# Narrow attention: one bank for the last four heads' queries and keys, and one maximum over the rows of two heads

## The reference

```
q = (x @ wq).reshape(b, n, heads, 16)    # heads = 20
k = (ctx @ wk).reshape(b, j, heads, 16)
v = (ctx @ wv).reshape(b, j, heads, 16)
a = softmax(q k^T * 16 ** -0.5)          # 512 x 512 per head
out = (a v) @ wo + bo
```

## Time and profile before

| | |
|---|---|
| median of 3 runs | 3327.07 us (3326.29 to 3332.21) |
| the profiled execution | 3336.34 us, its span 3334.6 us |
| PE busy | 3214.7 us, 96% of the span |
| DVE / ACT / POOL busy | 1737.4 / 1476.5 / 805.1 us |
| run r3, first column product at | 1817.8 us |
| run r7, first column product at | 2982.4 us |
| a self round (round 1), 1904.2 to 1994.7 | 90.5 us |
| a cross round (round 5), 2260.2 to 2347.3 | 87.1 us |

### The profile page before, as it was taken

How to read it: one execution, slowest core, us unless ns; L and a number is a source line. 1 busy time by engine, 2 the same in 40 slices (tenths; PEclk the granted TensorE clock), 3 DMA queues, 4 the chain that set the end, 5 groups by cost and what they waited for, 6 DMA issues and landing times.

```text
span 3334.6 us, 39289 instructions
## 1 busy us (share of the span) xinstructions
PE 3214.7 (96%) x15478; PEld 1462.8 (44%) x15478; DVE 1737.4 (52%) x2568; ACT 1476.5 (44%) x1983; POOL 805.1 (24%) x620
## 2 busy tenths in 40 slices
PE   7999999999999999999999999999999999989997
PEld 3344344443434343435444344444434545643443
DVE  2645455454555555552234677777762222656664
ACT  3544444445454545441112656666652112326664
POOL 2544444454554554550000000000000000000000
PEclk9999999999999999999999999999999999989999
DMA  3000000000100000000000000000002000000000
GB/s 110 24 16 20 16 17 20 23 19 20 58 18 18 17 23 13 16 24 20 0 5 26 1 1 1 30 11 6 1 23 65 1 0 33 1 5 6 14 9 17
DMA packets 37284, 62.32 MB, mean 19 GB/s; under 512 B 7024, under 2 KB 24944, under 8 KB 36208
## 3 DMA queue, kind: packets, MB, share of 16 engines
q1 hardware_dynamic: 37104, 59.82, 5.9%
HBM read 57.19 MB, written 2.62 MB: 18 GB/s over the span
## 4 chain that ended last, share of the span: by engine, by line
PE 89%; DVE 5%; ACT 4%; issue 1%; POOL 0%; DMA 0%; ACTq 0%; DVEq 0%; POOLq 0%
PE bank L1589 9%; PE bank L510 9%; PE bank L595 9%; PE bank L1126 7%; PE bank L737 5%; PE bank L351 5%; PE bank L673 5%; PE bank L1059 4%; PE bank L1251 3%; PE bank L676 3%; PE bank L709 3%; PE bank L1276 3%; PE bank L1179 2%; PE bank L533 2%; DVE heads L1084 2%; PE bank L1594 2%
## 5 line engine op out<-in xcount | busy, mean ns | idle before, releaser
L1084 DVE TENSOR_REDUCE heads<-bank 128x1 f32<-128x512 f32 x960 | 598.3, 683 | 237.2 <-PE bank L1072 236.4
L544 DVE TENSOR_REDUCE heads<-bank 128x2 f32<-128x1024 f32 x320 | 392.4, 1226 | 594.7 <-PE bank L533 594.7
L581 POOL TENSOR_TENSOR heads<-heads,probs 128x1024 f32<-128x1024 f32 x160 | 389.5, 2434 | 12.5
L567 ACT ACTIVATE probs<-bank 128x1024 f32<-128x1024 f32 x320 | 328.0, 1025 | 130.3 <-PE bank L519 130.0
L577 POOL TENSOR_TENSOR heads<-probs 128x1024 f32<-128x1024 f32 x80 | 190.7, 2384 | 712.8 <-ACT probs L567 712.8
L510 PE MATMUL bank<-heads 64*128 64x512 f32 x1280 | 335.7, 602 | 0.1
L1059 PE MATMUL bank<-heads 32*128 32x512 f32 x1920 | 296.8, 628 | 25.8 <-ACT weights L1097 10.9
L595 PE MATMUL bank<-probs,values 128*64 128x512 f32 x1280 | 294.0, 601 | 1.4 <-ACT nmT L558 1.0
L1589 PE MATMUL bank<-hT,weights 128*128 128x512 f32 x640 | 291.8, 606 | 1.5 <-issue 1.5
L1097 ACT ACTIVATE weights<-bank 128x1024 f32<-128x1024 f32 x236 | 228.8, 1022 | 96.0 <-PE bank L1059 93.9
L1652 ACT ACTIVATE ctx_in<-bank,b_col 128x512 f32<-128x512 f32 x80 | 55.1, 688 | 419.4 <-PE bank L1594 323.8
(11 more groups left out here) (205 smaller groups left out, 4868.9 us busy)
## 6 DMA issues: line engine op xcount, KB each, us to landing
heads<-in_wqk SPq DMA_DIRECT2D x40, 320.0 KB, 2.8
heads<-in_wqk SPq DMA_DIRECT2D x40, 256.0 KB, 2.6
weights<-in_L_xattn_w_ff SPq DMA_DIRECT2D x3, 1600.0 KB, 7.2
weights<-in_L_xattn_ff_w SPq DMA_DIRECT2D x3, 1600.0 KB, 7.1
ctx_in<-in_ctx SPq DMA_DIRECT2D x12, 384.0 KB, 3.7
weights<-in_L_xattn_qkv_q SPq DMA_DIRECT2D x2, 1632.0 KB, 7.4
weights<-in_L_xattn_wo SPq DMA_DIRECT2D x2, 1600.0 KB, 12.2
x_res<-in_x SPq DMA_DIRECT2D x4, 640.0 KB, 13.3
```

Of the source, the lines that this page charges most:

```text
L544: nc.vector.tensor_reduce(v["negm"][:, U % 2, qb, :].rearrange("p (g k) -> p g k", g=2)[:, :, 0], M.ROWS[:, :, :], AX.X, ALU.max, negate=T ...
L567: nc.scalar.activation(v["probs"][:, kb, :, :], M.COLS[kb % 2][:, :, :], ACT.Exp, scale=float(r.work[n][0].prm["dh"]) ** -0.5).then_inc(r. ...
L581: nc.gpsimd.tensor_tensor(ps, ps, pr[:, k, :, :], ALU.add).then_inc(r.sem("part"), 1)
L1084: nc.vector.tensor_reduce(v["negm"][:, tile, qb, 32 * h + at:32 * h + at + 1], r.bank_of(item, m)[:, :], AX.X, ALU.max, negate=True).then_ ...
```

## The change

Two things change, and with them the way banks are dealt out.

**Queries and keys of the last unit together.** Q2 and K2 become one item QK2 at step 0. Its products take 64 columns of wq into partitions 0 to 63 and 64 columns of wk into partitions 64 to 127 of the same bank, in turn (`QK_pe4`). ScalarE makes both tiles by four instructions on 64 partitions, and only the last of them releases the bank (`QK_act4`). V3 moves from step 0 to step 2, and what waited for K2 now waits for V3.

**Rows of two heads together.** A row item is now a pair of heads: two products into the two banks of a pair, one release to VectorE behind the second, and one maximum over 128 x 1024 that writes two values and releases both banks.

**Banks.** Banks 4 and 5 are pair 0, banks 6 and 7 pair 1. At step i the first row pair goes to pair i % 2, the second to the other, and the extra items alternate between the two single banks of pair i % 2. Counters: free0 to free3 for single banks, free4 and free5 for the pairs. A single item waits for its bank's counter and the pair's; a pair waits for its own and both single ones.

```
-    return [(f"row{i // 4}_{i % 4}_{h}", n) for h in range(4)] if 0 <= n < r.N else []
+    return [(f"row{i // 4}_{i % 4}_{p}", n) for p in range(2)] if 0 <= n < r.N else []
...
+        def choose(self, name, i):
+            if name[0:3] == "row":
+                self.large = 0
+                return 4 + (i + int(name[7])) % 2
+            self.large = 1 - self.large
+            return 2 * (i % 2) + 1 - self.large
+
+        def shares(self, bank):
+            return ((4,), (4,), (5,), (5,), (0, 1), (2, 3))[bank]
...
             self.wait(pe, f"free{bank}", k)
+            for other, count in self.beside[item, n]:
+                self.wait(pe, f"free{other}", count)
...
             if i == 0 and now:
-                items += [("Q2", n), ("V3", n)]
+                items += [("QK2", n)]
...
             if i == 2 and now:
-                items += [("K2", n)]
+                items += [("V3", n)]
...
+                r.wait_free(pe, item, m)
+                for g in range(2):
+                    strip = slice(64 * p + 32 * g, 64 * p + 32 * g + 32)
+                    last = nc.tensor.matmul(r.bank_of(item, m)[:, g, :], v["QB"][strip, u, qb * P:qb * P + P], v["KB"][strip, u, :], start=True, stop=True)
+                last.then_inc(r.full(item, m), 1)
...
-                nc.vector.tensor_reduce(v["negm"][:, tile, qb, 32 * h + at:32 * h + at + 1], r.bank_of(item, m)[:, :], AX.X, ALU.max,
-                                        negate=True).then_inc(r.free(item, m), 1)
+                out = v["negm"][:, tile, qb, :].rearrange("p (g k) -> p g k", g=4)[:, 2 * p:2 * p + 2, at]
+                nc.vector.tensor_reduce(out, r.bank_of(item, m)[:, :, :], AX.X, ALU.max, negate=True).then_inc(r.free(item, m), 1)
...
+        def QK_pe4(pe, r, n):
+            s, v, bank = r.work[n][0], n_view(r, n), r.bank_of("QK2", n)
+            r.wait_free(pe, "QK2", n)
+            for e in range(3):
+                for home, name, x, ch in ((bank[0:64, :], "wq", M.hT, CH3), (bank[64:P, :], "wk", kvT(s), keys(s))):
+                    if e < len(ch):
+                        last = nc.tensor.matmul(home, v[name][0:ch[e][1], e, 256:320], x[0:ch[e][1], e, :], start=e == 0, stop=e == len(ch) - 1)
+            last.then_inc(r.full("QK2", n), 1)
+
+        def QK_act4(act, r, n):
...
+            low, high = slice(0, 64), slice(64, P)
+            for out, part, scale, bias in ((v["QT"], low, 0, 6), (v["KT"], high, 0, 3)):
+                nc.scalar.activation(out[low, 4, :], bank[part, :], ACT.Identity, bias=M.mask[part, bias:bias + 1], scale=M.mask[part, scale:scale + 1])
+            nc.scalar.activation(v["QT"][high, 4, :], bank[low, :], ACT.Identity, bias=M.mask[low, 6:7], scale=M.mask[low, 1:2])
+            nc.scalar.activation(v["KT"][high, 4, :], bank[high, :], ACT.Identity, bias=M.mask[high, 4:5], scale=M.mask[high, 1:2]).then_inc(r.free("QK2", n), 1)
...
-                rows_pe4(pe, r, n, i, (0, 1))
+                rows_pe4(pe, r, n, i, 0)
                 if now:
                     cols_pe(pe, r, n, i, (2, 3, 0, 1)).then_inc(r.sem("cols"), 1)
-                rows_pe4(pe, r, n, i, (2, 3))
+                rows_pe4(pe, r, n, i, 1)
```

More of the change, by code:

```diff
@@ L80, in __init__ @@
         self.bank = [self.pair[i // 2][:, i % 2, :] for i in range(6)]
-        self.bank += [ctx.enter_context(nc.psum_tensor(f"bank{i}", [P, 512], F32)) for i in (6, 7)]
+        self.pair.append(ctx.enter_context(nc.psum_tensor("bank6", [P, 2, 512], F32)))
+        self.bank += [self.pair[3][:, i, :] for i in range(2)]
         self.PJ = self.bank[0:2]
@@ L88, in __init__ @@
         self.TR = self.bank[7]
-        self.NX = self.bank[4:8]
+        self.NX = self.bank[4:8] + self.pair[2:4]
         self.XB = self.bank[6:8]
@@ L383, in __init__ @@
                 self.sems, self.name, self.banks = {}, name, banks
-                self.place, self.period, self.upto = {}, {}, {}
+                self.place, self.period, self.upto, self.beside = {}, {}, {}, {}
                 count = [0] * len(banks)
@@ L391, in __init__ @@
                             self.period[item] = steps * n + i
+                            self.beside[item] = [(k, count[k]) for k in self.shares(bank)]
                             count[bank] += 1
@@ L1060, in cols_pe, with rows_pe4 @@
             return last
[L1062 to L1073, removed]
+        def rows_pe4(pe, r, n, i, p):
+            for item, m in rows_items(r, n, i)[p:p + 1]:
+                u, qb = int(item[3]), int(item[5])
+                v = n_view(r, m)
+                if qb == 0 and p == 0:
+                    r.wait(pe, "q_cast", 5 * m + u + 1)
+                    r.wait(pe, "k_cast", 5 * m + u + 1)
+                r.wait_free(pe, item, m)
[3 more added lines that the diff above has]
+                last.then_inc(r.full(item, m), 1)
@@ L1075, in rows_dve4 @@
         def rows_dve4(dve, r, n, i):
-            for item, m in rows_items(r, n, i):
-                u, qb, h = int(item[3]), int(item[5]), int(item[7])
+            for p, (item, m) in enumerate(rows_items(r, n, i)):
+                u, qb = int(item[3]), int(item[5])
                 v = n_view(r, m)
-                if qb == 0 and h == 0:
+                if qb == 0 and p == 0:
                     r.wait_full(dve, f"negm{(2, 3, 0, 1, 4)[u]}", m if u in (2, 3) else m - 1)
-                tile, at = (2, 16 - 16 * (h // 2)) if u == 4 else (u % 2, 16 - 16 * (u % 2))
+                tile, at = (2, 16 - 16 * p) if u == 4 else (u % 2, 16 - 16 * (u % 2))
+                out = v["negm"][:, tile, qb, :].rearrange("p (g k) -> p g k", g=4)[:, 2 * p:2 * p + 2, at]
@@ L1103, in negm_pe4 @@
             r.wait_free(pe, item, n)
-            for h in range(4):
-                r.wait_out(pe, f"row{u}_3_{h}", n)
+            for p in range(2):
+                r.wait_out(pe, f"row{u}_3_{p}", n)
             for qb in range(TB):
@@ L1258, in Q_act4 @@
             r.wait_full(act, item, n)
-            for u, which in ((2 * c, 0), (2 * c + 1, 1)) if c < 2 else ((4, 2),):
+            for u, which in ((2 * c, 0), (2 * c + 1, 1)):
                 last = nc.scalar.activation(v["QT"][:, u, :], r.bank_of(item, n)[:, :], ACT.Identity, bias=M.mask[:, 6:7],
@@ L1265, in Q_pool4 @@
             v = n_view(r, n)
-            r.wait_full(pool, f"row{min(2 * c + 1, 4)}_3_3", n - 1)
-            r.wait_out(pool, f"Q{c}", n)
+            r.wait_full(pool, f"row{min(2 * c + 1, 4)}_3_1", n - 1)
+            r.wait_out(pool, f"Q{c}" if c < 2 else "QK2", n)
             for u in range(2 * c, min(2 * c + 2, 5)):
@@ L1291, in K_pool4 @@
             v = n_view(r, n)
-            r.wait_full(pool, f"row{min(2 * c + 1, 4)}_3_3", n - 1)
-            r.wait_out(pool, f"K{c}", n)
+            r.wait_full(pool, f"row{min(2 * c + 1, 4)}_3_1", n - 1)
+            r.wait_out(pool, f"K{c}" if c < 2 else "QK2", n)
             for u in range(2 * c, min(2 * c + 2, 5)):
                 nc.gpsimd.tensor_copy(v["KB"][:, u, :], v["KT"][:, u, :]).then_inc(r.sem("k_cast"), 1)
+        def QK_pe4(pe, r, n):
[7 more added lines that the diff above has]
+        def QK_act4(act, r, n):
+            v, bank = n_view(r, n), r.bank_of("QK2", n)
+            r.wait(act, "cols", 20 * n)
+            r.wait(act, "q_cast", 5 * n)
+            r.wait(act, "k_cast", 5 * n)
+            r.wait_full(act, "QK2", n)
+            low, high = slice(0, 64), slice(64, P)
[3 more added lines that the diff above has]
+            nc.scalar.activation(v["KT"][high, 4, :], bank[high, :], ACT.Identity, bias=M.mask[high, 4:5], scale=M.mask[high, 1:2]).then_inc(r.free("QK2", n), 1)
         def V_pe4(pe, r, n, t):
```

20 lines of the change are left out of this document (10 added, 10 removed).

## The result

The changed kernel takes 3434.74 us (median of 4 runs, 3433.47 to 3436.5) where the kernel before takes 3329.64 (4 runs beside it, 3326.29 to 3336.91). The ratio is 1.0313, 95% interval 1.0294 to 1.0332: about 105 us slower. The forecast was 3412, with a range to 3446: the right sign and the main mechanism, with 85 us more where 105 were measured. The two profiled executions differ by 97 us (spans 3431.7 and 3334.6).

The account below looks back on a forecast made before the run. TensorE, busy 3214.7 of 3334.6 us, and its waits were taken as the bound. Middle rounds 66, first and last rounds 16 and lead steps 3 gave +85 us on 3327: 3412, range 3372 to 3446.

Parts of the forecast that it names:

- TensorE and its waits are all that counts: Whole kernel: TensorE is 89% of the chain of waits, so every new wait of TensorE is paid in full.
- The tie of the extra work to a two-head maximum: Extra work waits for the step's first pair maximum: +0.50 us where VectorE was on time, +0.54 where late.
- Third items, steps 4 to 7: The third extra item waits for the first one's bank to be copied out by ScalarE: +1.8 us a round.
- QK2 on TensorE: Query and key column halves run side by side, saving K2's 2.57 us a self round, 1.73 a cross round.
- QK2's copies: Step 1's second row pair waits for four ScalarE copies taking 2.79 us; mix4 at T + 3.35, +2.07 us.
- Lead steps: Six steps before each run, with row products without columns: +1.5 us for each run, 3 in all.
- the hidden tie: Rival, chance 0.06: something later bounds TensorE's step nearly everywhere, so only the gains are left; say 3290 us.
- the serial column pairs: Rival, chance 0.07: QK2's column pairs do not overlap, so 24 us of K2 come back; 3436 us.
- rival 3: Longer first maximum delays VectorE's later work too, another 0.3 us in every second step; 3448 us, chance 0.12.
- Rival 4: Most of the tie is real, but copies and third items cost little; 3380 us, chance 0.13.
- TensorE's busy time: Whole kernel: TensorE's busy time should fall by some 20 us while the span grows.
- a cross round: A middle cross round was to take about 95.4 us, against 87.10 before.

Follow-up runs that it names:

- e_half: The changed kernel with each two-head maximum reading only the first 256 of 512 keys per head: 3362.62 us, ratio to the kernel before 1.0090.
- e_layout: The kernel before with only the changed kernel's bank rule, one head per maximum, Q2 and K2 apart: 3352.73 us, ratio 1.0058.
- e_qk_split: The kernel before with QK2, its two key copies on VectorE and two query copies on ScalarE: 3326.5 us, ratio 0.9978.
- e_qk: The kernel before with QK2 alone, all four copies on ScalarE, one head per maximum, banks in rotation: 3354.06 us, ratio 1.0064.
- e_qk_mixfirst: The kernel before with QK2, four copies on ScalarE, and mix4 of step 1 ahead of the second pair of row products: 3328.6 us, ratio 0.9987.
- e_between: The kernel before with QK2, four copies on ScalarE, and mix4 of step 1 between the row products of heads 2 and 3: 3324.06 us, ratio 0.9970.
- e_between_split: The kernel before with QK2, mix4 of step 1 between row products of heads 2 and 3, and key copies on VectorE: 3317.07 us, ratio 0.9949.
- e_split: The changed kernel with QK2's key copies on VectorE and query copies on ScalarE: 3425.58 us, ratio to the kernel before 1.0271.

## Why the prediction came out as it did

- **TensorE and its waits are all that counts:** right. VectorE's saved 29 us and ScalarE's added 19 show only where they release a bank.
- **The tie of the extra work to a two-head maximum:** right in mechanism, place and size: 0.50 and 0.54 us a step were forecast, 0.37 to 0.60 measured in most tied steps, and e_half took 72 us away with the length of the maximum alone. In steps 11, 15 and 19 it was 0.35: their extra work starts 0.58 later, but what follows it comes closer behind (the second item after 0.47 us, before 0.60). In step 16 of rounds 9 and 10 it was 0.17. 46 us were forecast for the tied steps of the middle rounds, 41 measured.
- **Third items, steps 4 to 7:** right: 14 us of 14, and e_layout shows them alone (12 us there).
- **QK2 on TensorE:** right, side by side.
- **QK2's copies:** the term that was mis-sized. Steps 0 to 2 of the middle rounds were to give 6 us and gave 15. The step that failed is "four take 0.78 + 3 x 0.67 = 2.79": four took 3.13, the upper bound that the prediction named, and mix4 started 0.39 later, 3 us over the eight rounds. The rest is mainly the slow clock after the wait, about 5 us in rounds 1, 6 and 10, of which the prediction had nothing. What decides which rounds run slow stays open.
- **Lead steps:** +3 forecast, +9 measured; I had taken 1.5 a run without working it out. Most of it is the length of the maximum: in e_half the two lead stretches take 44.5 and 34.0 us (before 44.5 and 31.7), in the changed kernel 49.4 and 35.6. The other 2 us, in the second run, come with the bank rule (33.6 in e_layout).
- **Rivals:** the hidden tie and the serial column pairs did not occur. The added lateness of rival 3 did not occur either, as the tied steps cost 5 us less than forecast; the time lay near its number for other reasons. Rival 4 fails as well, since the third items cost all that was forecast.
- **TensorE's busy time:** "some 20 us" less was forecast, and it was 43, for the reason given above. It changes nothing in the sum, which goes by start times.
- **Luck:** a cross round of 95.25 us where 95.4 were forecast is better than the working deserves. In round 5 the tied steps cost 0.5 us less than forecast and steps 0 to 2 cost 0.3 more; the two nearly cancel.

## What to carry to other kernels

When a buffer is handed back by the consumer, a larger operation gives it back later: one maximum over two banks saves 5% of the engine's own time and holds the first bank 0.54 us longer, and where the producer is the bound, 0.35 to 0.60 us of that was paid at most uses here. Before halving a producer's work, look at who empties its result and what is queued behind them: an estimated 24 us saved on TensorE cost 46, most of it in the step that waited for four copies in a row, until work of another kind stood between. And replay one step with measured durations: that gave 4.44 us for step 6 where 4.41 were measured.

## What was not expected of the hardware

- Four ScalarE instructions on 64 partitions, alternating between partition halves, take 0.77 us each and 3.13 together; two on 128 partitions take 1.45 together. The alternation is not the reason: the two query copies of e_qk_split read the same half, and they take 1.56 together as well.
- After TensorE had stood idle for 2.0 to 2.5 us, the next mix ran with the granted clock at a mean of 0.76 in some rounds and at full clock in others of the same kernel: 4 of 10 in the changed kernel, 5 of 10 in e_half, 6 of 10 in e_qk. When the idle time was covered (e_qk_mixfirst, e_between, e_between_split), none did. With two shorter waits before the mix it went either way: 0.67 and 0.33 us, none slow (e_qk_split); 0.76 and 0.83 us, 2 of 10 slow (e_split). So the length of one wait does not settle it, and no run here shows what does.
- A maximum over 128 x 1024 took 1.220 us, and one over 128 x 512 in two banks 0.690, like one over a single bank of 512 (0.683): the length goes by elements, not by banks.
